# Block attention and a gated feed-forward layer on one core: scores from two 64-row halves in plain fp32, the expert product after the next projection, and matmul operands on 64-byte boundaries

## The reference, cut to what matters

```python
# x: 2 sequences x 2048 tokens x 1024
x3 = conv1d(x, conv_w, width=3, 'SAME') + conv_b            # 768 features: q, k, v of 256 each
q, k, v = split(x3); blocks of 128 tokens (32 blocks)
qh, kh, vh = q@wq + bq, k@wk + bk, v@wv + bv                # 16 heads of 64
p = softmax(causal(qh @ kh.T / 8))                          # inside a block of 128 tokens
o = (p @ vh) @ wo + bo
x = layernorm(x + o @ proj_w + proj_b)
base = x @ W_base.T + b_base                                # 1024 -> 1024
gate = softmax(x @ W_gate.T); thr = sigmoid(x @ W_thr.T + b_thr) / 8
wts = max(gate - thr, 0) / sum                              # 8 experts
moe = ((x @ A.T) * wts) @ B * 2                             # rank 16 per expert, 128 in all
x = layernorm(x + base + moe)
```

## Time and profile before

| what | us |
|---|---|
| median of 3 runs (1789.06 to 1789.9) | 1789.1 |
| the profiled execution, its own time | 1788.9 |
| its span, first to last instruction | 1787.1 |
| TensorE busy | 1721.5 |
| VectorE busy | 1435.8 |
| ScalarE busy | 721.7 |
| GpSimd busy | 332.2 |

### The profile page before, as it was taken

How to read it: one execution, slowest core, us unless ns; L and a number is a source line. 1 busy time by engine, 2 the same in 40 slices (tenths; PEclk the granted TensorE clock), 3 DMA queues, 4 the chain that set the end, 5 groups by cost and what they waited for, 6 DMA issues and landing times. The chain is left out here.

```text
span 1787.1 us, 32713 instructions
## 1 busy us (share of the span) xinstructions
PE 1721.5 (96%) x11712; PEld 1564.7 (88%) x11712; DVE 1435.8 (80%) x3281; ACT 721.7 (40%) x1881; POOL 332.2 (19%) x276
## 2 busy tenths in 40 slices
PE   5899999899999799999999999989999999999998
PEld 5899999899999688888888888868888888888887
DVE  8977679977777698888888888887777777777785
ACT  4333334332324477777777777751111111111110
POOL 6100003300000110100100102052333333333331
PEclk9999999999999899999999999999999999999999
DMA  4323222432242201010110111141112111121211
GB/s 140 115 77 100 77 82 100 142 106 78 89 158 88 77 1 48 1 47 8 39 47 0 47 47 53 63 134 55 67 53 79 53 72 60 60 72 53 77 41 48
DMA packets 48805, 123.03 MB, mean 69 GB/s; under 512 B 5489, under 2 KB 13681, under 8 KB 48241
## 3 DMA queue, kind: packets, MB, share of 16 engines
q1 hardware_dynamic: 48752, 122.36, 20.7%
HBM read 88.79 MB, written 33.55 MB: 68 GB/s over the span
## 5 line engine op out<-in xcount | busy, mean ns | idle before, releaser
L388 PE MATMUL conv_acc<-x_split,weights 128*128 128x256 f32 x4608 | 555.9, 283 | 32.0 <-DVE weights L314 24.6
L388 PEld LDWEIGHTS conv_acc<-x_split,weights 128*128 128x128 f32 x4608 | 552.7, 190 | 35.0 <-DVE weights L314 26.2
L1343 PE MATMUL ps_f<-weights 128*128 128x266 f32 (+2 forms) x1728 | 328.0, 342 | 0.0
L1343 PEld LDWEIGHTS ps_f<-weights 128*128 128x128 f32 x1728 | 279.6, 189 | 26.1
L247 ACT ACTIVATE x_split<-x_mixed 128x1024 fp32r<-128x1024 f32 x128 | 135.7, 1060 | 306.7 <-PE conv_acc L388 276.9
L309 DVE TENSOR_TENSOR x_split<-x_mixed,x_split 128x1024 fp32r<-128x1024 f32 x128 | 159.0, 1242 | 100.9 <-ACT x_split L247 100.8
L720 ACT ACTIVATE scores_and_probs<-scores_and_probs,score_neg_max 128x128 f32<-128x128 f32 x512 | 197.8, 392 | 4.2 <-DVE score_neg_max L831 4.2
L1179 ACT ACTIVATE gate_exp<-h_and_gate,gate_neg_max 128x8 f32<-128x8 f32 x32 | 9.6, 301 | 409.0 <-DVE gate_neg_max L1254 409.0
L683 POOL TENSOR_TENSOR weights<-conv_tile,weights 128x1024 fp32r<-128x1024 f32 x14 | 36.0, 2573 | 453.5 <-ACT weights L703 365.5
L826 DVE CUSTOM_DVE_ANT_0 scores_and_probs<-ps_scores,causal_mask 128x128 f32<-128x128 f32 x512 | 117.7, 285 | 0.5
L1343 PE MATMUL ps_f<-q_k_pairs,weights 128*128 128x266 f32 (+2 forms) x576 | 116.1, 337 | 0.0
(11 more groups left out here) (118 smaller groups left out, 2592.7 us busy)
## 6 DMA issues: line engine op xcount, KB each, us to landing
x_raw<-in_xT SPq DMA_DIRECT2D x128, 257.0 KB, 2.7
conv_tile<-in_x SPq DMA_DIRECT2D x32, 512.0 KB, 3.4
out<-out_tile SPq DMA_DIRECT2D x32, 512.0 KB, 2.6
convT_scratch<-features_out SPq DMA_DIRECT2D x16, 768.0 KB, 3.5
conv_tile<-convT_scratch SPq DMA_DIRECT2D x16, 768.0 KB, 6.4
conv_w_raw<-in_conv_w SPq DMA_DIRECT2D x16, 576.0 KB, 4.0
weight_stage<-in_ffn_w SPq DMA_DIRECT2D x8, 581.0 KB, 3.8
yT_scratch<-features_out SPq DMA_DIRECT2D x8, 512.0 KB, 3.7
```

The source lines that it names most:

```text
L388: last = nc.tensor.matmul(acc[f][k // 2][:, k % 2, :], w[:, c, a, k, f * P:(f + 1) * P], xs[:, c % XS, b, k, :], start=(c == 0 and k % 2 = ...
L1343: mm = nc.tensor.matmul(ps_f[par][n][:, 0:b0 - a0], x1T[:, par, a, kc, :], wf[kc][:, b, a0:b0], start=(kc == 0 and k == 0), stop=(n == 2 a ...
```

## The change

1. **Scores.** q and k become plain fp32 buffers (`q_and_k`), without the zeros and without a low part. Each block takes two matmuls, one for each head: head 0 from rows 0 to 63, head 1 from rows 64 to 127, 128 columns each, and each head has its own PSUM bank. 12 matmuls become 8. `qk_out` on VectorE goes, `k_out` on ScalarE is one instruction instead of two, the memsets go. `scores_done` is now raised twice at the end of the group instead of after blocks 1 and 3. The order of the eight maps is by head first, and the transposes read them so.
2. **Order in the feed-forward window.** `project` of i+2 comes ahead of `experts` of i.
3. **Places.** Weight slabs have a pitch of 1168 columns instead of 1162; slabs 6 and 7 have a buffer of their own; `x_split` is allocated ahead of `x_mixed` and `x_raw`; `o_bias` takes 16 columns; `h_weighted_T` and `thr_b` change places.

```diff
+WPITCH = -(-WCOLS // 16) * 16
-        self.stages = sb("weight_stage", [P, 2 * WCOLS], F32)
+        self.stages = sb("weight_stage", [P, 2 * WPITCH], F32)
-        xraw = sb("x_raw", [P, XS, 2, PAIRS + 1], F32)
+        xs = sb("x_split", [P, XS, 2, PROD, PAIRS], F32R)
         xmix = sb("x_mixed", [P, 2, PROD, PAIRS], F32)
-        xs = sb("x_split", [P, XS, 2, PROD, PAIRS], F32R)
...
+        xraw = sb("x_raw", [P, XS, 2, PAIRS + 1], F32)
...
-        pair = sb("q_k_pairs", [P, k_cols + q_cols], F32R)
+        qk = sb("q_and_k", [P, 2, 2, ST], F32)
+        self.k, self.q = qk[:, 0, :, :], qk[:, 1, :, :]
+        late = sb("late_weights", [P, self.LATE * 2 * WPITCH], F32R)
-        self.wf = [parts(wq + 2 * WCOLS * k, WCOLS) for k in range(kept)]
+        self.wf = [padded(attn.arena, wq + 2 * WPITCH * k) for k in range(kept)]
+        self.wf += [padded(late, 2 * WPITCH * k) for k in range(self.LATE)]
...
-                    nc.gpsimd.memset(k[rows(1 - j), i, :, :, j, :].bitcast(F32), 0.0).then_inc(k_zeroed, 1)
...
-                nc.scalar.activation(q[:, s % 2, HI, :], ps_qt[:], ACT.Identity, bias=bq[:, s:s + 1]).then_inc(q_hi, 1)
+                nc.scalar.activation(q[:, s % 2, :], ps_qt[:], ACT.Identity, bias=bq[:, s:s + 1]).then_inc(q_ready, 1)
...
-                for j in range(2):
-                    nc.scalar.activation(k[rows(j), s % 2, HI, :, j, :], ...).then_inc(k_hi, 1)
+                nc.scalar.activation(k[:, s % 2, :], ps_kt[:], ACT.Identity, bias=bk[:, s:s + 1]).then_inc(k_ready, 1)
...
-            def qk_out(g, s):
...
                 for b in range(BLK):
-                    for i, (a, c) in enumerate(PASSES):
-                        last = nc.tensor.matmul(ps_s[b // 2][:, b % 2 * 2 * P:(b % 2 + 1) * 2 * P],
-                                                q[:, s % 2, a, b * P:(b + 1) * P], k[:, s % 2, c, b, :, :],
-                                                start=(i == 0), stop=(i == 2))
-                    if b % 2 == 1:
-                        last.then_inc(s_done, 1)
+                    cols = slice(b * P, (b + 1) * P)
+                    for j in range(2):
+                        last = nc.tensor.matmul(ps_s[j][:, cols], q[rows(j), s % 2, cols], k[rows(j), s % 2, cols],
+                                                start=True, stop=True)
+                        if b == BLK - 1:
+                            last.then_inc(s_done, 1)
...
                 base(i, par, 1, range(CC // 2, CC))
-                experts(i, par)
                 if not last(n, 2):
                     project(i + 2, par)
+                experts(i, par)
```

More of the change, by code:

```diff
@@ L199, in _ @@
                         sp.dma_start(attn.craw[:, i * SF:(i + 1) * SF, :], convT[i * NST]).then_inc(attn.c_loaded, 16)
-                    for b, src in ((attn.bq, q_bias), (attn.bk, k_bias), (attn.bv, v_bias.partition_broadcast(P)),
+                    for b, src in ((attn.bq[:], q_bias), (attn.bk[:], k_bias), (attn.bv[:], v_bias.partition_broadcast(P)),
                                    (attn.bo, o_bias)):
-                        sp.dma_start(b[:], src).then_inc(attn.bias_loaded, 16)
+                        sp.dma_start(b, src).then_inc(attn.bias_loaded, 16)
                 unit(NST - 1, None, NST * sweep + NST - 1)
@@ L437, in parts, with padded @@
             return attn.arena[:, a:a + 2 * n].rearrange("p (i n) -> p i n", i=2)
-        k_cols, q_cols = 2 * 2 * BLK * 2 * P, 2 * 2 * ST
-        pair = sb("q_k_pairs", [P, k_cols + q_cols], F32R)
-        self.k = pair[:, 0:k_cols].rearrange("p (i h b j n) -> p i h b j n", i=2, h=2, b=BLK, j=2)
-        self.q = pair[:, k_cols:].rearrange("p (i h n) -> p i h n", i=2, h=2)
+        def padded(buf, a):
+            return buf[:, a:a + 2 * WPITCH].rearrange("p (i n) -> p i n", i=2)[:, :, 0:WCOLS]
+        qk = sb("q_and_k", [P, 2, 2, ST], F32)
+        self.k, self.q = qk[:, 0, :, :], qk[:, 1, :, :]
+        late = sb("late_weights", [P, self.LATE * 2 * WPITCH], F32R)
         wq, kept = attn.start[attn.WQ], CC - self.LATE
         self.wp = [parts(attn.start[attn.WV] + 2 * DM * k, DM) for k in range(KC)]
-        self.wf = [parts(wq + 2 * WCOLS * k, WCOLS) for k in range(kept)]
-        self.wf += [pair[:, 2 * WCOLS * k:2 * WCOLS * (k + 1)].rearrange("p (i n) -> p i n", i=2) for k in range(self.LATE)]
+        self.wf = [padded(attn.arena, wq + 2 * WPITCH * k) for k in range(kept)]
+        self.wf += [padded(late, 2 * WPITCH * k) for k in range(self.LATE)]
         self.wb = parts(attn.start[attn.WO] + 2 * attn.NW, DM)
@@ L451, in __init__ @@
         self.x1T = attn.arena[:, wo:wo + 4 * DM].rearrange("p (i h k n) -> p i h k n", i=2, h=2, k=CC)
-        self.stage = [attn.stages[:, i * WCOLS:(i + 1) * WCOLS] for i in range(2)]
-        self.stage.append(sb("weight_stage2", [P, WCOLS], F32)[:])
+        self.stage = [attn.stages[:, i * WPITCH:i * WPITCH + WCOLS] for i in range(2)]
+        self.stage.append(sb("weight_stage2", [P, WPITCH], F32)[:, 0:WCOLS])
         f = [(ffn_w[k], self.wf[k], WCOLS) for k in range(CC)]
@@ L961, in transpose_probs @@
                     for b in range(BLK):
-                        last = nc.tensor.transpose(out[:, b * P:(b + 1) * P], probs[:, s % 2, 2 * b + j, :], ident[:])
+                        last = nc.tensor.transpose(out[:, b * P:(b + 1) * P], probs[:, s % 2, j * BLK + b, :], ident[:])
                     last.then_inc(t_done, 1)
```

19 lines of the change are left out of this document (3 added, 16 removed).

## The result

The kernel after takes 1765.45 us (median of 4 runs, 1765.01 to 1767.22), the kernel before beside it 1789.5 (1789.06 to 1792.86): ratio 0.9863, 95% interval 0.9846 to 0.9881. Faster, but by 24 us where I had forecast 72; 1765 lies above my range of 1700 to 1753. The profiled execution of after was the slowest of its four, 1767.22 us; its span is 1765.3, 21.8 less than the profiled one of before.

The account below looks back on a forecast made before the run. TensorE was taken to bound convolution and attention, a TensorE-VectorE loop the feed-forward. Savings of 51.0 + 1.9 + 3 + 14.8 + 1 = 71.7 us from 1788.9 gave 1717 us, range 1700 to 1753.

Parts of the forecast that it names:

- Scores: Attention: fp32 row-half scores take 0.67 us a pair instead of 1.52, saving 0.85 over 60 pairs, 51.0 us.
- per pair of halves: Attention scores: two overlapping fp32 row halves cost 0.11 us, at most 0.128, priced from weighing v.
- Rival 1: Attention scores: halves in turn, or each pair at 0.22; group 1.11 us, total 1747 us; chance 0.30.
- Waits for the low part of q: Near attention's end: two waits of the transposes for q's low part vanish, 1.9 us.
- Start of attention: VectorE's small scaling slips ahead of GpSimd's subtraction or nothing changes: 0 to 7 us, taken as 3.
- Order: Feed-forward: project ahead of experts removes TensorE's wait, window 18.0 us, saving 14.8 us, bounds 5 to 15.
- rival 4: Feed-forward keeps its period because VectorE's 17.7 us of work grows: 1732 us; chance 0.05.
- Places: Buffer placements: 1 us gained in the feed-forward, 0 in the convolution.
- 0 for the convolution: Convolution: placing x_split changes nothing; 0.003 lower spacing would give 15 us, 0.002 higher cost 9.
- the 18.55 us of part 2: Feed-forward: today's window period as VectorE's chain 15.32, experts 1.61 and half of project 1.6 us.
- 2 (slower): Attention scores: full-width fp32 price, row halves in turn; 0.232 a half, group 2.09 us, total 1805; chance 0.07.
- 3 (placement helps the convolution): Convolution: placement gains 15 us more, total 1702 us; chance 0.08.

Follow-up runs that it names:

- heads_in_turn: Kernel after with the eight score calls ordered by head, all four blocks of head 0, then of head 1: 1794.79 us.
- scores_only: Kernel before with only the fp32 row-half scores, q and k in their own buffer, later buffers moved 2240 bytes: 1771.13 us.
- gpsimd_later: Kernel after with GpSimd's 4.50 us subtraction for the low part of wo waiting until the third v block is in SBUF: 1760.51 us.
- swap_alone: Kernel before with only project put ahead of experts in the feed-forward: 1777.46 us.
- before_x_on: Kernel before with 32 bytes of padding before and after x_split, so it alone starts on a 64-byte boundary: 1796.84 us.
- no_placement: Kernel before with the new scores and project ahead of experts, without the placements, buffers behind q and k moved 2240 bytes: 1757.03 us.
- x_plus_64: Kernel after with GpSimd's subtraction later and x_split 64 bytes up: 1751.3 us.
- place_map: Kernel after plus TensorE-only groups before the convolution, one per pair of moving-operand and weight starts; settled spacings read, its time is not the kernel's.
- place_probe: Kernel after plus a TensorE-only stretch before the convolution, varying the moving operand's start, then the weights'; spacings read, its time is not the kernel's.

## Why the prediction was wrong, step by step

**Scores: sign and mechanism right, price wrong.** The step that failed is "per pair of halves that is at most 0.128 us; I take 0.11 per pair". It took the 16 instructions of weighing v for 16 matmuls in 8 pairs. They are 8 calls in 4 pairs, so the very row I relied on says (1.02 - 0.14) / 4 = 0.22 a pair. With 0.22 my own sum gives 4 x 0.22 + 0.23 = 1.11. The group measured 1.09. The count was to be had: x1024 in the earlier trace rows over 64 pairs is 16, and the code calls 8. Rival 1 stood for this in its second wording, "each pair of halves at 0.22", though its 1747 us is not what came; its first wording, halves in turn at 0.11, fell with heads_in_turn, where a half costs 0.223 and the group 1.64.

The period fell by 0.274 and not by the 0.41 of rival 1. The group gave 1.52 - 1.09 = 0.43. The last projection before it takes 0.09 longer, since its step to the new tile shape is 0.318 us where it was 0.226; I had counted a change before the group, but within the 1.11. The remaining 0.07 went into 512-column matmuls, 231 to 232 ns apart in the projections of q and k and 229 in `add_out`, where all three were at 227. scores_only has the same period, so part 3 does not cause it. But there too `heads_out` and the buffers around it lie elsewhere modulo 256 than in before, and the matmuls of `add_out`, which read it, stand 233 ns apart there. Whether the new scores or the moved buffers do it, no run separates. Over 61 pairs 0.274 is 16.7 us, where I had 51.0.

**Waits for the low part of q:** gone, 1.9 us as forecast. **Start of attention:** forecast 3, a coin between 0 and 7. The stall stayed (5.17 us after 5.09): VectorE did not slip ahead, GpSimd started at 612.38, the second scaling at 613.08. From the first scores to the fourth, the three periods aside, after gains 1.2 us and loses 1.5 ahead of them to the clock. gpsimd_later shows the 5 us that lay there.

**Order: right.** Forecast 14.8 and a window of 18.0; measured 18.05 and 18.08, 18.02 without the placement, and swap_alone is 12.5 us faster. In before the first and the last windows were shorter than 18.56 already (18.26, 18.4), so all of them together give 13.1, and the entry at clock 0.50, which I had not thought of and which before_x_on has without the change, takes 2 back. VectorE's loop did not keep the pace (rival 4 falls).

**Places: wrong sign.** "0 for the convolution" rested on two rows that looked equal, 118 and 120 ns. That difference *was* the effect: 1.7 ns x 4608 is 7.7 us. I had even written "0.002 higher costs 9" and left it out of the range and the rivals, which held only the gain. (The 15 us beside it, for 0.003 lower, should have been 14, and the 18.55 us of part 2 add up to 18.53; neither matters here.) For the feed-forward I took 1 us of gain; no_placement shows a loss of about that size.

**The sum anew,** between the two spans. Attention: 17.2 over 58 pairs (15.9 from the period, 1.3 where the longer of the two waits for q stood; the other, 0.6, was in the last two), 2.0 over the first three, 1.4 over the last two, less 1.5 and 1.3 at its ends to the clock: 17.8. The feed-forward 13.1 - 2, the convolution -7.1: 21.8 in all. Of the 50 us that my 71.7 had too many, some 26 are the price of a pair of halves (60 x 0.44), 8 what lies around the scores in a pair, 8 the places, 2 the start of attention, 4 the windows and the entry, 3 the clock in attention; the last two pairs gave 1 that I had left out.

The other rivals: 2 (slower) had the price of a half nearly right, 0.232 against 0.223, and falls because the halves overlap. heads_in_turn, with half of the overlap gone, is slower than before, 1794.79 against 1790.35, though its group is 1.64 and not the 2.09 of that rival. 3 (placement helps the convolution) has the sign wrong for this change, but its 15 us and more are there for another start.

## What to carry to other kernels

Count a row's instructions against the calls in the code before taking a price per piece from it: an fp32 matmul shows as two. If small fp32 matmuls use half the rows, order them so that neighbours use different halves. And treat the place of a moving operand as something to measure, for example with a short stretch of matmuls at several starts: a boundary of 64 bytes is no rule, what counted was mostly the difference of the two starts modulo 256, and the spread here, 113 to 120 ns, was worth 27 us, nearly as much as the 33 of the scores and the order together.

## What the hardware showed that I had not expected

- The spacing of 256-column fp32r matmuls that load 128 weight columns each depends on where moving operand and weights start: 113.3 to 120.0 ns with TensorE alone, with a period of 256 bytes (one group of eight, at 0, did not repeat: 118.6 and 120.0) and, in 59 of 64 groups, by the difference of the two starts alone. The kernel under load shows the probe's value to 0.1 ns, x_plus_64 that of place_map.
- One pair of starts can have two steady spacings, 113.3 ns in place_probe and 117.7 in place_map and x_plus_64. What makes a run fall into one of them is not known; x_plus_64 had four runs at 1751 to 1754 us and one, not profiled, at 1740.
- fp32 row halves of the array work at the same time: 0.22 us for two calls as for one, their instructions starting 6 ns apart.
- Behind a stall of 5.2 us TensorE worked for some us at a clock of 0.50, 1.9 us on top of the waiting; with a stall of 1.5 us the clock stayed at 1.00 (gpsimd_later).
- A 4.5 us GpSimd operation stretches a 128x4 scaling on VectorE from 0.17 to 3.82 us, and a normalization over 128x1024 from 1.22 to 3.31 us, while the masked maxima beside it kept 0.28, the addition from PSUM that writes `v_heads` 0.69 and a reciprocal of 128x8 0.19. The scaling ends at 616.90, with GpSimd's operation at 616.88, so it is held to the end rather than slowed.
